# A five-layer graph network on one core: six turned blocks of the adjacency matrix are turned again on VectorE instead of being stored

## The chip, the core and the metric

The kernel runs on one core of one Trainium2 chip. The metric is the device time of one execution in microseconds (us). "PE" is TensorE, "DVE" VectorE, "ACT" ScalarE, "POOL" GpSimd and "SP" SyncE; SP does nothing here but issue transfers and wait for the semaphores before them.

## What is computed

A chain of four layers on x (5120 nodes by 64 features) with a dense 5120 by 5120 matrix adj, all in float32:

```
h = relu(layernorm(x));  x = x + L0(h): e = (weights and diagonal applied to h) + h
                                        layernorm(adj @ (adj.T @ e)) * gamma + beta + h
h = relu(layernorm(x));  x = x + adj @ h                                   # L1
h = relu(layernorm(x));  T1 = adj @ h; T2 = 2 adj @ T1 - h; T3 = 2 adj @ T2 - T1
                         x = x + h W0 + T1 W1 + T2 W2 + T3 W3 + b          # L2
h = relu(layernorm(x));  x = x + relu(d (adj + I) d (h W + b)), d = degree ** -0.5   # L3
```

adj is 105 MB and doesn't fit on the chip. A product adj @ v contracts over the columns of adj, so TensorE needs it turned (columns on the partitions).

## The kernel before

**First stage.** adj is read once, in seven groups of columns (six of 768, one of 512), ten blocks of 512 rows each, into `raw`. TensorE uses each block for adj.T @ e (`products_for_t`, L651) and turns it 128 by 128 with an identity (`turn_banks`, L673); ScalarE copies the turned banks into `staged` (`copy_banks`, L879). Of the six 128-wide chunks of a pair of blocks VectorE turns the last (`turn_chunk`, L1129), with instructions of 32 by 256 that each turn 32 by 32 squares. The turned pair (3 MB: three tiles of 1 MB) serves for the second product of L0 (`product_for_h`) and is stored to `adj_t` in DRAM (`store`, L570). The last group stays on the chip as far as it fits.

**Five passes.** The rest is five products with adj: one for L1, three for L2, one for L3. A tile (m, k) is 256 columns k by 1024 rows m, turned: 1 MB, in one of the slots of `whole`. A pass has 5 rows m of 20 tiles. A tile costs TensorE 8 matmul instructions (`multiply`, L640), and one that is loaded is used for the next pass too, as a "dual", where the features of that pass are ready in time. `Plan` writes this out by hand as 334 steps: in each the own tile, the small matmuls that belong to the ends of rows, then the duals of the step. All engines run through the same steps, each in its own order, and meet only at semaphores. 305 tiles are used and 295 of these loaded, in plan order, by SP (`load_turned`, L588); a load waits until the tile that was in its slot has been multiplied. `Plan` gives a tile the slot that comes free first. Fifteen slots rotate, some of them available only later: `over_wide` (slot 0), ten of `over_last` and four in `staged`; three more serve once. Eight tiles (`AT_START`) are loaded before the passes begin, the first of them into slot 0.

**Ends of rows.** A row that ends with its own tile at step e is finished by VectorE: at step e+1 it copies the sum out of the bank (L1243 with a part, L1245 without) and turns it with 16 small transposes (L1169), except in the fourth pass and in the last row of all, where TensorE does that (L799) and waits for the copy. At e+2 the result goes into x or into the features of the next pass (L1215, L1221, L1226, L1229 to L1234). After the passes of L1 and L2's last product a normalisation follows: at e+3 and e+4 on VectorE, ScalarE and POOL (the last instruction of it is L1203 in the first pass), then for the first pass L809 on TensorE at e+7 and a copy on ScalarE (L995) in the same step, and two batches of weights on TensorE (L825) at e+8 and e+9, which VectorE reads (L1184, L1188) and ScalarE too (L1005). TensorE doesn't begin the second batch before the first has been read. For the fourth pass these come at e+5 and e+6 (L809, L831, L1194, L1197).

How soon features are used is fixed by `READY = [11, 4, 4, 8, None]`: a row of pass p that ended at step e has its features ready for pass p+1 at step e + READY[p], and TensorE waits for `rows_ready` there.

Of the kernel before, what the change touches and what calls it, by code (L numbers as in the profile page):

```python
# [10 lines left out]
P = 128  # L11
# [28 lines left out]
SLOTS = EARLY_SLOTS + NB + LATE_SLOTS  # L40
KEPT = CHUNKS_LAST // 2
ONCE = SLOTS + KEPT
AT_START = [0] + list(range(EARLY_SLOTS + NB, SLOTS)) + [ONCE] + list(range(EARLY_SLOTS + NB - KEPT, EARLY_SLOTS + NB))
OPEN_BANKS = 5
EPS = 1e-5
SQ = 32
# [20 lines left out]
WEIGHED = (0, 3)  # L67
KEPT_FROM = 12
EARLY_FROM, EARLY_EVERY, EARLY_ROWS = 2, 2, 2


def kept_slot(m, j):
# [4 lines left out]
class Plan:  # L77


    def __init__(self):  # L80
# [114 lines left out]
        for n, (p, m, k, _) in enumerate(self.tiles):  # L195
            if p == 0 and k >= COLS - KEPT:
                self.slot[n] = kept_slot(m, k - (COLS - KEPT))
                if m >= 1:
                    empty.append((self.used_no(n), self.slot[n], n))
        loads_of = {}  # L200
        for n in range(len(self.tiles)):
            if n not in self.slot:
                place = min(empty, key=lambda x: x[0])
                empty.remove(place)
                _, j, self.slot_before[n] = place
                loads_of[j] = loads_of.get(j, 0) + 1
                self.slot[n], self.load_no[n] = j, loads_of[j]
                self.loads.append(n)
                if j != ONCE:
                    empty.append((self.used_no(n), j, n))  # L210

    def early_in_row(self, order, m, left, step, ready, covered):

# [23 lines left out]
def gnn_stack(nc, x_d, adj_d, wu_d, du_d, pu_d, wi_d, di_d, pi_d, gam_d, bet_d, w2_d, b2_d, w3_d, b3_d, out_d):  # L237
    plan = Plan()
    ctx = ExitStack()
    with ctx:  # L240
# [3 lines left out]
        def sem(name):  # L244
            return ctx.enter_context(nc.semaphore(name))
# [50 lines left out]
        over_c12 = [c12_flat[:, j * TILE_WORDS:(j + 1) * TILE_WORDS] for j in range(KEPT)]  # L296
        over_y = staged[:, LATE_SLOTS * TILE_WORDS:(LATE_SLOTS + 1) * TILE_WORDS]
        whole = [w[:, :] for w in over_wide + over_last] + over_staged + over_c12 + [over_y]
        out_rows = sq
        C1, C2 = C12[:, 0], C12[:, 1]  # L300

# [19 lines left out]
        early_in = sem("early_in")  # L321
        late_in = sem("late_in")
        weights_ready = sem("weights_ready")
        x_in = [sem(f"x_in{i}") for i in range(len(X_PARTS))]
        diag_in = sem("diag_in")
        diag_turned = sem("diag_turned")
# [44 lines left out]
        pool_step = sem("pool_step")  # L371

        adj_v = adj_d.rearrange("(m a p) k -> p m a k", a=SUB, p=P)
        x_v = x_d.rearrange("(t p) d -> p t d", p=P)
        out_v = out_d.rearrange("(m a p) d -> p m a d", a=CH, p=P)
        FEATURES = [R, E, C2, C1, R]
# [36 lines left out]

        def wait_loaded(eng, n):

            if n in plan.load_no:
                eng.wait_ge(whole_in[plan.slot[n]], 16 * plan.load_no[n])

        def chunks(g):
# [129 lines left out]
        @block.sync  # L549
        def _(sp):  # L550
            def load_x(i):
                t = slice(X_PARTS[i][0] * SUB, X_PARTS[i][1] * SUB)
                sp.dma_start(X[:, t, :], x_v[:, t, :]).then_inc(x_in[i], 16)

            def load_first(m):
                sp.dma_start(raw[:, m], adj_v[:, m, :, 0:GW]).then_inc(raw_in[m], 16)

            load_x(0)
            sp.dma_start(diag_rows[0:U // P, :], du_d.rearrange("(t p) -> t p", p=P)).then_inc(diag_in, 16)
            sp.dma_start(diag_rows[U // P:NT, :], di_d.rearrange("(t p) -> t p", p=P)).then_inc(diag_in, 16)  # L560
            load_x(1)
            load_first(0)
            load_x(2)
            for m in range(1, NB):
                load_first(m)

            def store(g, m):
                wait_copied(sp, g, m)
                at = g * CHUNKS * PAIR
                sp.dma_start(adj_t[m, :, at:at + STAGE_WORDS], staged_pair(g, m)).then_inc(stored_by(g, 2 * m)[0], 16)  # L570

            def store_kept(u):
                wait_copied(sp, NG - 1, u // 2, u % 2)
                at = (NG - 1) * CHUNKS * PAIR + u % 2 * TILE_WORDS
                sp.dma_start(adj_t[u // 2, :, at:at + TILE_WORDS], turned_into(NG - 1, u)).then_inc(stored_by(NG - 1, u)[0], 16)

            def load_next(g, m):

                wait_turned(sp, g, m // 2)
                wait_summed(sp, g, m)  # L580
                src = adj_v[:, m, :, (g + 1) * GW:(g + 1) * GW + chunks(g + 1) * P]
                sp.dma_start(raw_of(g + 1, m), src).then_inc(raw_in[m], 16)

            def load_turned(n):

                p, m, k, dual = plan.tiles[n]
                j = plan.slot[n]
                sp.dma_start(whole[j], adj_t[m, :, k * TILE_WORDS:(k + 1) * TILE_WORDS]).then_inc(whole_in[j], 16)  # L588

            def first_load(n):  # L590
                p, m, k, dual = plan.tiles[n]
                g = (2 * k + 1) // CHUNKS
                for u in (2 * m, 2 * m + 1):
                    sp.wait_ge(*stored_by(g, u))
# [12 lines left out]
            first = iter(plan.loads[:len(AT_START)])  # L607
            first_load(next(first))
            sp.wait_ge(*stored_by(NG - 2, UNITS - 3))
            sp.wait_ge(used, unit_no(NG - 2, UNITS - 2))  # L610
            for _ in range(STAGE_WORDS // TILE_WORDS):
                first_load(next(first))
            store_kept(0)
            store_kept(1)
            sp.wait_ge(*stored_by(NG - 2, UNITS - 1))
            sp.wait_ge(used, unit_no(NG - 1, 0))
            for _ in range(LATE_SLOTS + 1 - STAGE_WORDS // TILE_WORDS):
                first_load(next(first))
            for u in range(2, UNITS):
                if u == UNITS - 1:  # L620
                    wait_turned(sp, NG - 1, u // 2)
                    wait_summed(sp, NG - 1, u)
                    for n in first:
                        first_load(n)
                store_kept(u)
            for u in range(UNITS - 2, UNITS):
                sp.wait_ge(*stored_by(NG - 1, u))
            sp.wait_ge(used, TOTAL_UNITS)
            for n in plan.loads[len(AT_START):]:
                sp.wait_ge(multiplied, plan.used_no(plan.slot_before[n]))  # L630
                load_turned(n)
# [216 lines left out]
        def _(act):  # L848
# [129 lines left out]
                group(g)  # L978
            last_group()

            for s in range(N_STEPS):
                if UNITS + s <= END_V:
                    end_of_layer(UNITS + s)
# [24 lines left out]
                for r in plan.row_at(s, 4, 4):  # L1008
                    p, m = plan.rows[r]
                    act.wait_ge(out_ready, m + 1)  # L1010
                    act.dma_start(out_v[:, m], out_rows[m % 2][:, :, :]).then_inc(out_stored[m % 2], 16)
            for i in range(2):
                act.wait_ge(out_stored[i], 16 * len(range(i, ROWS, 2)))

# [2 lines left out]
        def _(dve):  # L1017
# [143 lines left out]
            def turn_squares(r):  # L1161
# [8 lines left out]
                                                       src[q * SQ:(q + 1) * SQ, :, b, :])  # L1170
                last.then_inc(y_squares, 1)

            for s in range(N_STEPS):
                if UNITS + s <= END_V:
                    end_of_layer(UNITS + s)
# [59 lines left out]
                for r in plan.row_at(s, 1, *range(PASSES)):  # L1235
                    p, m = plan.rows[r]
                    dve.wait_ge(multiplied, plan.own_no[plan.last_own[p, m]])
                    if r - 2 in BY_TENSOR:
                        dve.wait_ge(y_rows, BY_TENSOR.index(r - 2) + 1)
                    bank = open_bank[plan.bank["own", p, m]]  # L1240
                    if (p, m) in plan.part_no:
                        dve.wait_ge(part_saved, plan.part_no[p, m] + 1)
                        ins = nc.vector.tensor_tensor(y_sb[r % 2], bank, part[:, m, :], ALU.add)  # L1243
                    else:
                        ins = nc.vector.tensor_copy(y_sb[r % 2], bank)  # L1245
                    ins.then_inc(y_saved, 1)
                    if r in BY_VECTOR:
                        dve.wait_ge(y_saved, r + 1)
                        turn_squares(r)


        @block.gpsimd
# [70 lines left out]
```

## Time and profile before

| | |
|---|---|
| median of 3 runs | 1450.26 us (1450.21 to 1451.71) |
| the profiled execution: its time, and the span in its trace | 1449.24 us, 1447.0 us |
| busy: PE, DVE, ACT, POOL | 1419.3 us (98%), 491.5 us (34%), 399.7 us (28%), 84.2 us (6%) |
| mean granted clock of TensorE | 0.999 of full speed |
| moved by DMA | 523.26 MB, mean 362 GB/s |
| first stage, five passes | 0 to about 549 us, 549 to 1447 us |

The span goes from the first to the last instruction; the time has some 2 us more around it. Busy shares are means over two stages that differ. Matmuls are pipelined and their ends modelled, so a busy PE isn't proof of a PE at its peak: the waits and the chain of work that ended last say who held whom.

### The profile page before, as it was taken

What the parts mean: (1) busy time and instruction counts of PE and PEld (TensorE: products, weight loads), DVE (VectorE), ACT (ScalarE), POOL (GpSimd) and SP (SyncE); (2) the same over time, 40 slices, a digit from 0 to 9 for tenths busy, and PEclk for the clock granted to TensorE, in tenths of its full rate; (3) what the DMA queues carried; (4) which work ended last, traced back from release to release, by engine and by line L of the source; (5) the groups of instructions that cost most, each with busy time, mean ns of one, the idle gap of its engine ahead of it and who ended that gap; (6) DMA issues with size and microseconds to landing.
All of it is one profiled execution on the core that took longest, in us unless ns stands there. A gap on an engine that the chain in (4) does not pass through costs nothing.

```text
span 1447.0 us, 18473 instructions
## 1 busy us (share of the span) xinstructions
PE 1419.3 (98%) x7601; PEld 600.1 (41%) x7601; DVE 491.5 (34%) x1082; ACT 399.7 (28%) x885; POOL 84.2 (6%) x67
## 2 busy tenths in 40 slices
PE   6999999999999999999999999999999999999998
PEld 3555555555555563333333333333333333333332
DVE  6684544545546533331132211011311121101044
ACT  2378777777776551000000000000000000000000
POOL 2210000000000037000000000000000000000000
PEclk9999999999999999999999999999999999999999
DMA  9999999999999998999996797899797848996998
GB/s 322 392 417 411 420 412 414 419 408 415 401 406 372 388 403 348 419 421 420 420 413 217 315 361 291 327 350 319 302 340 263 311 180 354 393 382 224 357 420 315
DMA packets 97607, 523.26 MB, mean 362 GB/s; under 512 B 18764, under 2 KB 18804, under 8 KB 54644
## 3 DMA queue, kind: packets, MB, share of 16 engines
q1 hardware_dynamic: 90436, 520.40, 91.3%
q10 hardware_dynamic: 7088, 1.67, 0.5%
q8 instruction: 61, 1.00, 0.3%
q14 instruction: 22, 0.18, 0.0%
HBM read 415.88 MB, written 106.17 MB: 361 GB/s over the span
## 4 chain that ended last, share of the span: by engine, by line
PE 61%; DMA 2%; DVE 1%; POOL 0%; issue 0%; ACT 0%; DVEq 0%
PE turned L640 33%; PE acc L640 25%; DMA over_wide<-adj_t 2%; PE turned L673 1%; PE turned L825 1%; PE t_rows L809 0%; PE turned L831 0%; DVE staged L1169 0%; PE t_acc L799 0%; PE t_acc L725 0%; PE t_rows L725 0%; POOL rstd L1272 0%; DVE staged L1035 0%; DVE staged L1025 0%; DVE staged L1231 0%
## 5 line engine op out<-in xcount | busy, mean ns | idle before, releaser
L1129 DVE STREAM_TRANSPOSE staged<-raw 32x256 f32<-32x256 f32 x448 | 194.9, 435 | 5.8
L651 PE MATMUL t_acc<-raw,E 128*64 128x384 f32 (+1 forms) x1120 | 184.4, 476 | 5.7 <-DMA raw<-in_adj_dram 5.7
L879 ACT ACTIVATE staged<-turned 128x512 f32<-128x512 f32 x303 | 152.7, 640 | 105.7 <-PE turned L673 105.2
L923 ACT ACTIVATE t_t<-raw 128x768 uint8<-128x768 f32 (+1 forms) x216 | 177.2, 902 | 0.0
L640 PE MATMUL acc<-staged,t_cur 128*64 128x512 f32 x720 | 161.1, 596 | 0.0
L673 PE MATMUL turned<-ident,raw 128*128 128x128 f32 x1376 | 160.2, 274 | 0.0
L673 PEld LDWEIGHTS turned<-ident,raw 128*128 128x128 f32 x1376 | 149.7, 140 | 24.9 <-issue 24.9
L640 PE MATMUL turned<-over_last,C 128*64 128x512 f32 x672 | 152.1, 592 | 0.0
L651 PEld LDWEIGHTS t_acc<-raw,E 128*64 128x64 f32 x1120 | 78.3, 138 | 109.4 <-issue 86.0
L1272 POOL TENSOR_TENSOR rstd<-rstd,minus_half 128x8 f32<-128x8 f32 (+1 forms) x30 | 44.2, 1473 | 1267.1 <-DVE rstd L1031 1267.1
L640 PE MATMUL turned<-over_last,R 128*64 128x512 f32 x512 | 116.5, 593 | 0.0
L640 PE MATMUL acc<-over_last,R 128*64 128x512 f32 x440 | 99.9, 593 | 0.0
L987 ACT ACTIVATE part<-turned 128x512 f32<-128x512 f32 x12 | 7.2, 597 | 313.1 <-PE turned L640 287.3
L1169 DVE STREAM_TRANSPOSE staged<-staged 32x128 f32<-32x128 f32 x304 | 91.9, 302 | 4.5
L640 PEld LDWEIGHTS turned<-over_last,C 128*64 128x64 f32 x672 | 48.2, 137 | 95.5 <-issue 95.5
L1083 DVE TENSOR_TENSOR h_acc<-acc,h_acc 128x512 f32<-128x512 f32 x30 | 20.8, 692 | 197.2 <-PE acc L640 197.2
L640 PEld LDWEIGHTS acc<-staged,t_cur 128*64 128x64 f32 x720 | 49.0, 137 | 90.8 <-issue 90.8
L640 PE MATMUL acc<-over_last,C 128*64 128x512 f32 x384 | 86.6, 592 | 0.0
L1243 DVE TENSOR_TENSOR staged<-turned,part 128x512 f32<-128x512 f32 x11 | 7.6, 692 | 225.8 <-PE turned L640 191.7
L640 PE MATMUL turned<-over_last,E 128*64 128x512 f32 x320 | 74.1, 593 | 0.0
L640 PEld LDWEIGHTS turned<-over_last,R 128*64 128x64 f32 x512 | 36.2, 137 | 71.2 <-issue 69.4
L855 ACT ACTIVATE staged<-staged 128x512 f32<-128x512 f32 x10 | 6.3, 630 | 206.0 <-DVE staged L1025 206.0
(139 smaller groups left out, 1062.9 us busy)
## 6 DMA issues: line engine op xcount, KB each, us to landing
over_last<-adj_t SPq DMA_DIRECT2D x181, 1024.0 KB, 8.9
staged<-adj_t SPq DMA_DIRECT2D x91, 1024.0 KB, 9.5
raw<-in_adj_dram SPq DMA_DIRECT2D x60, 1536.0 KB, 19.7
adj_t<-staged SPq DMA_DIRECT2D x30, 3072.0 KB, 18.1
over_wide<-adj_t SPq DMA_DIRECT2D x23, 1024.0 KB, 7.6
raw<-in_adj_dram SPq DMA_DIRECT2D x10, 1024.0 KB, 14.8
adj_t<-over_last SPq DMA_DIRECT2D x8, 1024.0 KB, 12.1
adj_t<-C SPq DMA_DIRECT2D x2, 1024.0 KB, 21.7
```

The costliest lines, as they stand in the source:

```text
L640: last = nc.tensor.matmul(bank[h * D:(h + 1) * D, :], v[:, t + c, :], tile[:, (2 * c + h) * B:(2 * c + h + 1) * B], start=start and c == 0 ...
L651: last = nc.tensor.matmul(t_acc[h * D:(h + 1) * D, 0:columns], E[:, m * SUB + a, :], raw_of(g, m)[:, a, h * columns:(h + 1) * columns], st ...
L673: last = nc.tensor.transpose(turned[n % TURN_BANKS][:, a * P:(a + 1) * P], raw_of(g, 2 * m + b)[:, sub, c * P:(c + 1) * P], ident[:, :])
L825: last = nc.tensor.matmul(weigh_bank[odd][:, i * 4 * D:(i + 1) * 4 * D], feat_t[rows, nodes], w0123[rows, :, :].rearrange("p w d -> p (w d ...
L879: nc.scalar.activation(turned_into(g, u)[:, i * B:(i + 1) * B], turned[n % TURN_BANKS][:, :], ACT.Copy) \
L923: nc.scalar.activation(passed[n % 2][:, 0:chunks(g) * P], raw_of(g, m)[:, a, :], ACT.Copy, accum_out=deg_part[:, m * SUB + a, g:g + 1]).th ...
L987: nc.scalar.activation(part[:, m, :], open_bank[plan.bank["dual", p, m]], ACT.Copy).then_inc(part_saved, 1)
L1083: ins = nc.vector.tensor_tensor(h_acc[:, m, :], acc[pair % 2][:, :], h_acc[:, m, :], ALU.add)
L1129: last = nc.vector.transpose(dst[b * SQ:(b + 1) * SQ, :, :, q * SQ:(q + 1) * SQ], src[q * SQ:(q + 1) * SQ, :, :, c * P + b * SQ:c * P + (b ...
L1169: last = nc.vector.transpose(dst[b * SQ:(b + 1) * SQ, :, h, e, :], src[q * SQ:(q + 1) * SQ, :, b, :])
L1243: ins = nc.vector.tensor_tensor(y_sb[r % 2], bank, part[:, m, :], ALU.add)
L1272: op.tensor_tensor(v, v, minus_half[:, t(0)], ALU.pow).then_inc(pow_ready, 1)
```

## The change

Six tiles, (m, k) = (2, 2), (4, 5), (3, 8), (4, 11), (3, 14) and (4, 17), each the last third of a stored pair, are left out of the store. TensorE, ScalarE and VectorE still turn them in the first stage, for the second product of L0. Where a pass has such a tile to load, ScalarE's queue loads two raw blocks of adj (1024 rows by 128 columns, 512 KB each, in rows of 512 bytes) into two rooms, and VectorE turns them into the tile's slot: 16 transposes a block, in four "quarters" of four, which `place_turning` assigns to steps, two quarters a step at most and none in the three steps after the end of a row. The rooms lie in `over_wide`, so slot 0 is gone for tiles, fourteen slots rotate and seven tiles are loaded ahead.

```diff
-AT_START = [0] + list(range(EARLY_SLOTS + NB, SLOTS)) + [ONCE] + ...
+AT_START = list(range(EARLY_SLOTS + NB, SLOTS)) + [ONCE] + ...
+UNSTORED = [(2, 2), (4, 5), (3, 8), (4, 11), (3, 14), (4, 17)]
+QUARTERS = 4
+QUARTERS_A_STEP = 2
+ROOM_LANDS, ROOM_AHEAD = 3, 6
...
-                loads_of[j] = loads_of.get(j, 0) + 1
-                self.slot[n], self.load_no[n] = j, loads_of[j]
-                self.loads.append(n)
+                self.slot[n] = j
+                if self.tiles[n][1:3] in UNSTORED:
+                    raws.append(n)
+                    self.turned_no[n] = 2 * len(raws)
+                else:
+                    loads_of[j] = loads_of.get(j, 0) + 1
+                    self.load_no[n] = loads_of[j]
+                    self.loads.append(n)
...
+    def place_turning(self, raws):
...
+        row_ends = {s + i for s in self.ended for i in (1, 2, 3)}
+        self.rooms_in, self.quarters_in, ends = {}, {}, []
+        for n in raws:
+            free = step_of[self.slot_before[n]][-1]
+            for c in range(2):
+                asked = max([free - ROOM_AHEAD] + [x + 1 for x in ends[-2:-1]])
+                self.rooms_in.setdefault(asked, []).append((n, c))
+                s = max([asked + ROOM_LANDS, free + 1] + ends[-1:])
+                q = 0
+                while q < QUARTERS:
+                    if s not in row_ends and len(self.quarters_in.get(s, [])) < QUARTERS_A_STEP:
+                        self.quarters_in.setdefault(s, []).append((n, c, q))
+                        q += 1
+                    else:
+                        s += 1
+                ends.append(s)
...
+        rooms = [over_wide[0][:, c * ROOM_WORDS:(c + 1) * ROOM_WORDS] for c in range(2)]
...
             def wait_loaded(eng, n):
-            if n in plan.load_no:
+            if n in plan.turned_no:
+                eng.wait_ge(room_turned, plan.turned_no[n])
+            elif n in plan.load_no:
...
             def store(g, m):
-                wait_copied(sp, g, m)
-                at = g * CHUNKS * PAIR
-                sp.dma_start(adj_t[m, :, at:at + STAGE_WORDS], staged_pair(g, m))...
+                at, words = g * CHUNKS * PAIR, STAGE_WORDS
+                if (m, (g + 1) * CHUNKS // 2 - 1) in UNSTORED:
+                    words = STAGE_WORDS - TILE_WORDS
+                    ... (waits for the banks of these words alone)
+                sp.dma_start(adj_t[m, :, at:at + words], staged_pair(g, m)[:, 0:words])...
...
             first = iter(plan.loads[:len(AT_START)])
-            first_load(next(first))
...
+            def load_room(n, c):                                  # on ScalarE, last in its step
+                p, m, k, dual = plan.tiles[n]
+                job = plan.turned_no[n] - 2 + c
+                if job >= 2:
+                    act.wait_ge(room_turned, job - 1)
+                at = k * 2 * P + c * P
+                act.dma_start(rooms[c].rearrange("p (r k) -> p r k", k=P),
+                              pair_v[:, m, :, at:at + P]).then_inc(room_in[c], 16)
...
+            def turn_room(n, c, q):                               # on VectorE, last in its step
+                if q == 0:
+                    dve.wait_ge(room_in[c], 8 * plan.turned_no[n])
+                    if c == 0:
+                        dve.wait_ge(multiplied, plan.used_no(plan.slot_before[n]))
+                src = rooms[c].rearrange("p (a h k) -> p h a k", h=2, k=P)
+                dst = whole[plan.slot[n]][:, c * PAIR:(c + 1) * PAIR].rearrange("p (h a n) -> p h a n", h=2, a=SUB)
+                for b in range(4):
+                    last = nc.vector.transpose(dst[b * SQ:(b + 1) * SQ, :, :, q * SQ:(q + 1) * SQ],
+                                               src[q * SQ:(q + 1) * SQ, :, :, b * SQ:(b + 1) * SQ])
+                if q == QUARTERS - 1:
+                    last.then_inc(room_turned, 1)
```

## Rows read from the trace of the kernel before

**Rows 1.** Windows: us, busy PE, PEld, DVE, ACT, POOL, granted clock, DMA share, GB/s.

```profile
216.00:252.00 36.00, 36.00 (x226) 18.66 (x224) 16.62 (x38) 29.11 (x68) 0.00 (x0) 1.00 1.02 411
612.00:648.00 36.00, 35.85 (x172) 12.02 (x168) 10.64 (x28) 2.59 (x5) 1.64 (x1) 1.00 1.01 420
```

**Rows 2.** Waits of PE over the span: total us, times, longest.

```profile
PE t_acc L651 <- DMA raw<-in_adj_dram: 5.7, 16, 1.0
...
PE acc L640 <- DMA over_wide<-adj_t: 0.2, 1, 0.2
```

**Rows 3.** Chain of work that ended last, first pass: start us, us, what.

```profile
581.75 14.55 DMA over_wide<-adj_t
...
648.45 0.41 PE turned L825
...
699.68 0.41 PE turned L825
...
700.75 39.63 PE acc L640 x184
...
757.78 0.41 PE turned L825
...
798.62 0.66 PE t_rows L809 x4
...
801.14 0.41 PE turned L825
```

**Rows 4.** Timeline of SP's queue where the passes begin.

```profile
555.15 0.32 SPq L588 DMA_DIRECT2D over_wide<-adj_t  x1
```

**Rows 5.** DMA of the last 67 us (1380 to 1447), ScalarE's queue.

```profile
q10 hardware_dynamic: 5200, 1.31, 8.6%
```

**Rows 6.** Costliest groups: count, busy us, mean ns of one, idle before.

```profile
L1129 DVE STREAM_TRANSPOSE staged<-raw 32x256 f32<-32x256 f32 x448 | 194.9, 435 | 5.8
```

**Rows 7.** Timeline of DVE, ends of four rows of the first pass.

```profile
642.66 0.68 DVE L1203 TENSOR_TENSOR X<-X,b 128x512 f32<-128x512 f32 x1
...
692.57 0.68 DVE L1203 TENSOR_TENSOR X<-X,b 128x512 f32<-128x512 f32 x1
...
750.67 0.68 DVE L1203 TENSOR_TENSOR X<-X,b 128x512 f32<-128x512 f32 x1
...
798.48 0.68 DVE L1203 TENSOR_TENSOR X<-X,b 128x512 f32<-128x512 f32 x1
```

**Rows 8.** Timeline of DVE, passes two to four.

```profile
1007.52 0.68 DVE L1222 SCALAR_TENSOR_TENSOR X<-staged,X 128x512 f32<-128x512 f32 x1
1014.89 0.69 DVE L1243 TENSOR_TENSOR staged<-turned,part 128x512 f32<-128x512 f32 x1 [6.68 <-PE turned L640]
...
1157.98 0.69 DVE L1226 SCALAR_TENSOR_TENSOR C<-staged,C 128x512 f32<-128x512 f32 x1
...
1245.15 0.69 DVE L1243 TENSOR_TENSOR staged<-turned,part 128x512 f32<-128x512 f32 x1 [27.93 <-PE turned L640]
```

**Rows 9.** Chain of work that ended last, fourth pass.

```profile
1167.58 0.59 PE t_acc L799 x4
...
1246.82 0.59 PE t_acc L799 x4
```

**Rows 10.** Timeline of DVE, last pass.

```profile
1382.61 0.69 DVE L1197 TENSOR_TENSOR R<-R,dis 128x512 f32<-128x512 f32 x1
...
1393.07 5.04 DVE L1169 STREAM_TRANSPOSE staged<-staged 32x128 f32<-32x128 f32 x16
...
1440.41 0.69 DVE L1243 TENSOR_TENSOR staged<-acc,part 128x512 f32<-128x512 f32 x1 [1.55 <-PE acc L640]
```

**Rows 11.** Windows, last 3 us, columns as in rows 1.

```profile
1444.00:1447.00 3.00, 0.00 (x0) 0.00 (x0) 0.00 (x0) 0.00 (x0) 0.00 (x0) 0.50 0.38 87
```

**Rows 12.** Timeline of PE at the start of the kernel.

```profile
17.48 4.22 PE L651 MATMUL t_acc<-raw,E 128*64 128x384 f32 x16
...
22.44 2.80 PE L651 MATMUL t_acc<-raw,E 128*64 128x384 f32 x16
```

More of the change, by code:

```diff
@@ L42 @@
 ONCE = SLOTS + KEPT
-AT_START = [0] + list(range(EARLY_SLOTS + NB, SLOTS)) + [ONCE] + list(range(EARLY_SLOTS + NB - KEPT, EARLY_SLOTS + NB))
+AT_START = list(range(EARLY_SLOTS + NB, SLOTS)) + [ONCE] + list(range(EARLY_SLOTS + NB - KEPT, EARLY_SLOTS + NB))
 OPEN_BANKS = 5
@@ L69 @@
 EARLY_FROM, EARLY_EVERY, EARLY_ROWS = 2, 2, 2
+UNSTORED = [(2, 2), (4, 5), (3, 8), (4, 11), (3, 14), (4, 17)]
+ROOM_WORDS = CH * P
+QUARTERS = 4
+QUARTERS_A_STEP = 2
+ROOM_LANDS, ROOM_AHEAD = 3, 6
 def kept_slot(m, j):
@@ L200, in __init__ @@
         loads_of = {}
+        self.turned_no, raws = {}, []
         for n in range(len(self.tiles)):
@@ L205, in __init__ @@
                 _, j, self.slot_before[n] = place
-                loads_of[j] = loads_of.get(j, 0) + 1
-                self.slot[n], self.load_no[n] = j, loads_of[j]
-                self.loads.append(n)
+                self.slot[n] = j
[6 more added lines that the diff above has]
+                    self.loads.append(n)
                 if j != ONCE:
                     empty.append((self.used_no(n), j, n))
+        self.place_turning(raws)
+    def place_turning(self, raws):
+        step_of = {}
+        for s, n in enumerate(self.step_tile):
+            for x in [n] * (n is not None) + self.duals_in.get(s, []):
+                step_of.setdefault(x, []).append(s)
+        row_ends = {s + i for s in self.ended for i in (1, 2, 3)}
[14 more added lines that the diff above has]
+                ends.append(s)
+            assert ends[-1] + 2 <= step_of[n][0], (self.tiles[n], ends[-1], step_of[n])
     def early_in_row(self, order, m, left, step, ready, covered):
@@ L323, in gnn_stack @@
         weights_ready = sem("weights_ready")
+        room_in = [sem(f"room_in{c}") for c in range(2)]
+        room_turned = sem("room_turned")
         x_in = [sem(f"x_in{i}") for i in range(len(X_PARTS))]
@@ L373, in gnn_stack @@
         adj_v = adj_d.rearrange("(m a p) k -> p m a k", a=SUB, p=P)
+        pair_v = adj_d.rearrange("(m r p) k -> p m r k", r=CH, p=P)
         x_v = x_d.rearrange("(t p) d -> p t d", p=P)
@@ L567, in store @@
             def store(g, m):
-                wait_copied(sp, g, m)
-                at = g * CHUNKS * PAIR
-                sp.dma_start(adj_t[m, :, at:at + STAGE_WORDS], staged_pair(g, m)).then_inc(stored_by(g, 2 * m)[0], 16)
+                at, words = g * CHUNKS * PAIR, STAGE_WORDS
+                if (m, (g + 1) * CHUNKS // 2 - 1) in UNSTORED:
+                    words = STAGE_WORDS - TILE_WORDS
+                    sp.wait_ge(chunk_copied, COPIED_NO[g, m, words // B - 1])
+                    if (g, m, MOVED_BANK) in MOVED_NO:
+                        sp.wait_ge(bank_moved, MOVED_NO[g, m, MOVED_BANK])
+                else:
+                    wait_copied(sp, g, m)
+                sp.dma_start(adj_t[m, :, at:at + words], staged_pair(g, m)[:, 0:words]).then_inc(stored_by(g, 2 * m)[0], 16)
             def store_kept(u):
@@ L979, in _ @@
             last_group()
+            def load_room(n, c):
[4 more added lines that the diff above has]
+                at = k * 2 * P + c * P
+                act.dma_start(rooms[c].rearrange("p (r k) -> p r k", k=P), pair_v[:, m, :, at:at + P]).then_inc(room_in[c], 16)
             for s in range(N_STEPS):
@@ L1011, in _ @@
                     act.dma_start(out_v[:, m], out_rows[m % 2][:, :, :]).then_inc(out_stored[m % 2], 16)
+                for n, c in plan.rooms_in.get(s, []):
+                    load_room(n, c)
             for i in range(2):
@@ L1249, in _ @@
                         turn_squares(r)
+                for n, c, q in plan.quarters_in.get(s, []):
+                    turn_room(n, c, q)
         @block.gpsimd
```

## Prediction

> **What bounds the kernel now.** The windows come first [rows 1]. In the first stage (216 to 252 us) the DMA engines are full, 411 GB/s at a share of 1.02, and TensorE is busy for all 36 us; early in the passes (612 to 648) the DMA is as full (420 GB/s) and TensorE busy 35.85 of 36. Two resources are at their limit at once, so busy shares don't say who holds whom. The waits do [rows 2]: TensorE stood for raw blocks 5.7 us in the whole run, in 16 pieces, for a turned tile 0.2 us in the row shown. TensorE is the bound, and the DMA is only just quick enough. How just, the chain shows [rows 3]: it runs through TensorE's matmuls, but at 581.75 it leaves them for a transfer of 14.55 us, whose landing lets TensorE go on. There a tile lands as it is needed; slack grows later. The same chain gives the unit: 184 matmuls in 39.63 us are 23 tiles, 1.72 us a tile. VectorE looks free (10.64 of 36 us in the second row of [rows 1]), but its work comes in clumps at the ends of rows, and there TensorE needs it: at 798.62 the chain [rows 3] steps from VectorE's last work to TensorE's L809 without a gap.
>
> **First stage.** Six of 30 stores lose 1 MB of 3. No instruction of TensorE goes, since all six tiles are still turned there. The DMA is relieved of 6 x 1.049 MB / 411 GB/s = 15.3 us [rows 1], but TensorE can get back only what it stood for: 5.7 us [rows 2]. I take -5.0, bounds 0 and -5.7.
>
> **Loads in the passes.** The planner's rules, followed in the code, replace 18 of 295 loads by 36 raw blocks. Two things press on the stretch without slack. First, slot 0 is gone: one tile fewer is loaded ahead, and since the stream of the passes starts at 555.15 as before [rows 4] (SP stands there for its last stores), 1 MB more must pass before each tile: 1.049 / 420 GB/s = 2.5 us. Second, the raw blocks of the first turning, (2, 2), are asked at step 38, which ScalarE reaches after its work of step 28, some 10 steps ahead of its slot; their MB passes before tiles that have no slack. Their price isn't in the trace: by bytes 2.5 us; by the 256-byte rows of the output, 8.6% of 16 x 67 us / 5200 = 17.7 ns a packet [rows 5], two such for each 512 bytes, 2048 x 35 / 16 ns = 4.5 us. A line through 17.7 ns and the 312 ns of an 8 KB packet at 420 GB/s gives 27 ns, 3.5 us, which I take since it leans on the nearer row. Together +6.0, bounds 2.5 (raw blocks absorbed) and 9. The Trainium skill (DMA: Bandwidth & Descriptors, Specifications) puts the least transfer at line rate at 512 bytes; by that the blocks would cost 2.5 us and the sum 1 us less. No run here shows it yet.
>
> **VectorE's price.** The new transposes have the shape of L1129, 32 by 256, 435 ns each [rows 6]: 16 a block, 6.96 us; 32 a tile, 13.92 us; 18 tiles 250 us, on an engine that is two thirds idle. But two quarters a step are 3.48 us, against 1.72 us for a step of one tile, and VectorE works in order: the end of a row waits behind every quarter of an earlier step. The planner spares only steps e+1 to e+3. Where steps hold an own tile and a dual (3.44 us) nothing happens. The other places, in order, with the times of before:
>
> - **Steps 48 and 68.** Four quarters stand between the end of normalisation (L1203) and VectorE's reading of the first batch, which TensorE needs for its second. L1203 ends at 643.34 and 693.25 [rows 7]; plus 6.96 and 0.95 for the reading: 651.25 and 701.2, where TensorE wants to go on at 648.45 and 699.68 [rows 3]. +2.8 and +1.5.
> - **Step 88.** Here eight quarters, those of tile (4, 11), lie in steps 83 to 86, between the same two. The quarters of steps 76 to 79 delay VectorE by 1.8 us, which the slack of the row nearly hides (0.2). L1203's end at 751.35 [rows 7] + 13.92 + 1.0 = 766.3, against 757.78 [rows 3]: 8.5, and with the 1.8 delay less the stall 0.2 already counted, +10.0 in all.
> - **Steps 106, 107.** Quarters in steps 98 and 99 need 6.96 us; the row's last tile is done 3 tiles (5.15 us) after they can start: 1.8 late, and L809 at 798.62 has no slack. Then the four of steps 103 and 104 follow L1203 (799.16 [rows 7] + 1.8) and end at 807.9. ScalarE, in step 105, waits for that very turning before it asks the next raw block, and the copy that L825 needs is behind it: 807.9 + 0.7 = 808.6 against 801.14 [rows 3] + 1.8. +1.8 and +5.6.
> - **Step 117.** With quarters in 107 to 110 the end of the next row starts 2.2 us late; its 0.3 of slack leaves +2.0.
> - **Step 180.** Eight quarters in steps 173 to 176, one tile each. VectorE is free for them at 1008.2 and would end at 1022.1; the row's copy stood at 1014.89 [rows 8]. 7.2 late, and the four tiles (6.9 us) that cover its 6.5 us of turning are the whole slack. +7.2.
> - **Step 224.** The same in steps 220 to 223: from 1158.67 [rows 8] to 1172.6, then a copy of 0.7: 1173.3. TensorE itself waits for it at L799, at 1167.58 [rows 9]. +5.8.
> - **Step 247.** Steps 241 to 244, started 6 tiles before the row's copy at 1245.15 [rows 8], at 1234.8: 1248.7 + 0.7 against 1246.82 [rows 9]. +2.6.
> - **The end.** From 1383.3 [rows 10] VectorE has three tiles to turn (41.8 us), four rows to finish at 0.7 + 5.04 + 3 x 0.7 = 7.9 us (31.6) and the last row's 6.6 us (1440.41 to 1447.0): 1463.3, where all of it lay beside TensorE before. TensorE meanwhile waits some 10 us for its last tile, inside this. +16.3.
>
> VectorE's sum: 2.8 + 1.5 + 10.0 + 7.4 + 2.0 + 7.2 + 5.8 + 2.6 + 16.3 = 55.6 us.
>
> **TensorE's clock.** It fell to 0.50, 1.2 GHz, in the last 3 us, when TensorE had nothing left [rows 11], so four stalls of over 5 us (88, 107, 180, 224) should bring it down. Coming back costs, by the first 16 matmuls of L651 after a thin stretch, 4.22 - 2.80 = 1.4 us [rows 12]: +5.6; bounds 0 and twice that, if those 16 were slow throughout.
>
> **Hidden.** ScalarE's 36 issues cost nothing where it waits anyway; without that cover 36 x 0.32 (SP's issue [rows 4]) = 11.5 us. SP has 18 issues fewer; its in-order waits gain nothing, since slots come free at TensorE's pace.
>
> Sum: -5.0 + 6.0 + 55.6 + 5.6 = 62.2. The profiled execution took 1449.24, so 1511.4; the median is 1.0 above it: 1512.
>
> **Rivals.** (1) *Not slower: VectorE's turning fits.* It decides at the price of a quarter: at 0.86 us, two in a step of one tile, VectorE keeps pace, the stalls at 88, 180 and 224 vanish and the end is covered. Then -5.0 + 6.0 is left, 1451, and with the bounds 5.7 and 2.5 taken, 1447. For it speaks that VectorE idles two thirds of the run; against it, 448 instructions of the same shape at 435 ns, twice that price [rows 6]. The Trainium skill (VectorE: DVE Perf Modes, The three transpose paths) gives 311 ns for 128 by 128 in bf16, an estimated 5.0 us for a tile's 16 such squares, and by that this rival would hold; the trace, in float32, says 13.92. (2) *Part of the lateness is absorbed:* stalls move TensorE behind, so that later clumps find VectorE ahead, or duals fill the gaps. With steps 88, the end and half of the others: 10.0 + 16.3 + 14.6 + 1 = 42, 1492; with no clock loss and the end halved, 1484. For it: one wait can hide another, as at step 224; against: the places lie 40 us and more apart, each with its own clump. (3) *The raw blocks land late.* VectorE then stands in order before a quarter. They are asked at least 3 steps (5.2 us) ahead; a full DMA took 14.55 us [rows 3]. If half of the 18 came 4 us late on the path, +36: 1548. Against it: nearly all are asked while VectorE is still busy with the block before, 7 us.
>
> **Chances.** Forecast 0.75; (1) 0.05; (2) 0.12; (3) 0.08. The likeliest gives 1512. Its own bounds: 1450.3 + 55.6 - 2.8 (step 48 absorbed) - 5.7 + 2.5 = 1500, and 1450.3 + 55.6 + 9 + 11.2 = 1526. With parts of (2) and (3): 1488 to 1535, which leaves out (1), the lower half of (2) and most of (3). A measurement tells 0.2% (3 us) from no change. Slower takes all of the forecast, (2) and (3), 0.95; (1) is split, 0.03 same and 0.02 faster.
>
> **What would show it.** Some 576 transposes of 32 by 256 at 435 ns, VectorE busy near 740 us; waits of L651 for raw blocks under 1 us; waits of TensorE for VectorE's new transposes, near 10 us at the last tile, and for the readings before L825 (10 us), for ScalarE's copy (5 to 6), at L799 (6) and for C at the duals of step 180 (7); the last 60 us full on VectorE. A wait for a raw block behind VectorE would be rival (3). The prediction is wrong if quarters are cheaper than 435 ns allow, or if the planner's order of VectorE isn't what I read.

## The result, and the profile after

The change makes the kernel slower: 1552.86 us against 1450.24 on the same chip (medians of four runs each), a ratio of 1.0705 with a 95% interval of 1.0692 to 1.0717. The forecast was 1512, its range 1488 to 1535; 62.2 us more were forecast and 102.6 came.

The profiled execution of the changed kernel took 1555.73 us, 106.5 more than that of before; its span is 1553.9 us and the mean granted clock 0.968 (before: 1447.0 and 0.999). The page comes first: busy time of the engines, two groups of instructions (operation, count, busy us, mean ns, idle time before them), and two kinds of transfer (count, size, median us to landing). Line numbers have moved: L640 is now L689, L651 L700, L799 L848, L809 L858, L825 L874, L1005 L1063, L1243 L1317; L1242 is the new turning, L1037 the new load.

```profile
PE 1443.3 (93%) x7601; PEld 606.0 (39%) x7601; DVE 743.0 (48%) x1658; ACT 400.0 (26%) x885; POOL 84.3 (5%) x67
...
L1242 DVE STREAM_TRANSPOSE over_last<-over_wide 32x256 f32<-32x256 f32 x416 | 181.3, 436 | 92.8 <-PE turned L689 67.0
...
L1242 DVE STREAM_TRANSPOSE staged<-over_wide 32x256 f32<-32x256 f32 x160 | 69.8, 436 | 46.9 <-DMA over_wide<-in_adj_dram 44.7
...
over_wide<-in_adj_dram ACTq DMA_DIRECT2D x36, 512.0 KB, 7.9
adj_t<-staged SPq DMA_DIRECT2D x6, 2048.0 KB, 15.5
```

The 576 transposes take 436 ns each, and VectorE is busy 743.0 us, both as forecast. TensorE issues the same 7601 matmuls, but is busy 24.0 us longer, and its idle time in the span (span less busy) went from 27.7 to 110.6 us: 82.9 + 24.0 = 106.9, the whole growth of the span. So there are two things to explain, waits and slower matmuls. First the waits. These are the waits of PE in the changed kernel (total us, times, longest), to be held against [rows 2]:

```profile
PE turned L689 <- DVE staged L1242: 14.7, 1, 14.7
PE t_acc L848 <- DVE staged L1317: 14.6, 3, 6.2
PE turned L874 <- ACT C L1063: 13.0, 3, 10.7
PE acc L689 <- DVE staged L1242: 11.2, 1, 11.2
PE acc L689 <- DVE over_last L1242: 9.4, 1, 9.4
PE acc L689 <- DVE C L1300: 7.6, 1, 7.6
PE t_rows L858 <- DVE staged L1095: 7.4, 3, 4.4
...
PE turned L874 <- ACT feat_t L1053: 5.1, 1, 5.1
PE t_acc L700 <- DMA raw<-in_adj_dram: 1.9, 2, 1.0
```

Most are the waits that were forecast. Two are not: the 11.2 us for a turned tile in the first pass (with 4.4 us behind it, at L858), and 14.7 beside the 9.4 near the end, where one wait of some 10 was expected. What VectorE did before those two, its timeline shows (start, us, instructions, in brackets the idle time before and what ended it):

```profile
674.22 7.18 DVE L1242 STREAM_TRANSPOSE staged<-over_wide 32x256 f32<-32x256 f32 x16 [16.86 <-DMA over_wide<-in_adj_dram]
694.02 7.18 DVE L1242 STREAM_TRANSPOSE staged<-over_wide 32x256 f32<-32x256 f32 x16 [12.62 <-DMA over_wide<-in_adj_dram]
...
1489.58 7.18 DVE L1242 STREAM_TRANSPOSE staged<-over_wide 32x256 f32<-32x256 f32 x16 [2.49 <-DMA over_wide<-in_adj_dram]
1509.45 7.18 DVE L1242 STREAM_TRANSPOSE staged<-over_wide 32x256 f32<-32x256 f32 x16 [12.69 <-DMA over_wide<-in_adj_dram]
```

VectorE stands for raw blocks four times, 44.7 us in all, and the turnings of the blocks that came late end where TensorE begins again. ScalarE's queue shows when these two blocks of the first pass were asked (the second line joins two issues, the first of which waits for nothing):

```profile
648.76 0.38 ACTq L1037 DMA_DIRECT2D over_wide<-in_adj_dram  x1
...
657.39 24.42 ACTq L1037 DMA_DIRECT2D over_wide<-in_adj_dram  x2
```

The block asked at 648.76 could be turned at 674.22, that of 657.39 at 694.02: 25 and 37 us, where the median block took 7.9 from issue to landing. The DMA queues from 657 to 695 us say why (packets, MB, share of 16 engines; q1 carries SP's loads of tiles, q10 the raw blocks of ScalarE's queue):

```profile
q1 hardware_dynamic: 1989, 14.48, 93.0%
q10 hardware_dynamic: 1988, 1.00, 9.2%
```

The two queues get the same number of packets, not of bytes: 1988 small ones and 1989 large ones. A small packet costs 9.2% x 16 x 38 us / 1988 = 28 ns, a large one 93.0% x 16 x 38 / 1989 = 284 ns. A raw block is 1024 rows of 512 bytes, 64 packets on each of 16 engines; if each waits for one large packet, a block takes an estimated 64 x (28 + 284) ns = 20 us. The two blocks came 19.8 us apart (674.22 and 694.02). The Trainium skill (DMA: Bandwidth & Descriptors, Queues, rings and completion order) says that an engine goes round its queues packet by packet; these rows agree.

TensorE's clock explains the rest. Windows around the wait before step 88's second batch, columns as in [rows 1]:

```profile
786.00:791.00 5.00, 0.00 (x0) 0.00 (x0) 4.83 (x12) 0.00 (x0) 0.00 (x0) 0.50 0.00 0
791.00:794.00 3.00, 2.02 (x10) 1.28 (x10) 0.80 (x4) 0.38 (x1) 0.00 (x0) 0.50 0.02 5
794.00:797.00 3.00, 3.00 (x10) 0.99 (x10) 0.89 (x4) 0.77 (x2) 0.00 (x0) 0.50 0.30 85
797.00:800.00 3.00, 3.00 (x14) 0.94 (x12) 0.00 (x0) 0.00 (x0) 0.00 (x0) 0.84 0.97 264
```

TensorE begins again at 791.98 and has 0.50, 1.2 GHz, until about 798; then 2.4 GHz come back. Matched one by one with those of the kernel before, the matmuls behind this wait are 3.0 us longer in sum. Behind each of ten waits of 2.2 to 14.7 us they are 1.3 to 3.2 us longer, 24.1 us together; behind the last wait of the run, which only four matmuls follow, 0.5; the rest of the run is 0.6 shorter. That is the 24.0.

### The profile page after: what moved, and what is told of

It is laid out like the page before. It is cut to its first block, busy times and chain, and to the rows that moved or that the text cites. A ratio compares the mean times of both kernels' runs of the same rounds, so it can differ in the third digit from the quotient of the medians.

```text
span 1553.9 us, 19071 instructions
## 1 busy us (share of the span) xinstructions
PE 1443.3 (93%) x7601; PEld 606.0 (39%) x7601; DVE 743.0 (48%) x1658; ACT 400.0 (26%) x885; POOL 84.3 (5%) x67
## 4 chain that ended last, share of the span: by engine, by line
PE 43%; DVE 15%; DMA 8%; issue 1%; POOL 0%; ACT 0%; ACTq 0%; DVEq 0%
PE turned L689 22%; PE acc L689 19%; DVE over_last L1242 7%; DMA over_wide<-in_adj_dram 5%; DVE staged L1242 3%; DMA staged<-adj_t 3%; DVE staged L1229 3%; PE turned L722 1%; PE turned L874 1%; POOL rstd L1348 0%; PE turned L880 0%; DVE staged L1317 0%; PE t_acc L848 0%; PE t_rows L858 0%; DVE staged L1319 0%
## 5 line engine op out<-in xcount | busy, mean ns | idle before, releaser
L1242 DVE STREAM_TRANSPOSE over_last<-over_wide 32x256 f32<-32x256 f32 x416 | 181.3, 436 | 92.8 <-PE turned L689 67.0
L700 PE MATMUL t_acc<-raw,E 128*64 128x384 f32 (+1 forms) x1120 | 182.4, 477 | 1.9 <-DMA raw<-in_adj_dram 1.9
L689 PE MATMUL acc<-staged,t_cur 128*64 128x512 f32 x720 | 161.1, 596 | 0.0
L689 PE MATMUL turned<-over_last,C 128*64 128x512 f32 x632 | 142.8, 592 | 0.0
L689 PE MATMUL turned<-over_last,R 128*64 128x512 f32 x560 | 131.3, 604 | 1.5 <-DMA over_last<-adj_t 1.5
L689 PE MATMUL acc<-over_last,R 128*64 128x512 f32 x472 | 112.7, 612 | 10.2 <-DVE over_last L1242 9.4
L700 PEld LDWEIGHTS t_acc<-raw,E 128*64 128x64 f32 x1120 | 79.7, 138 | 101.9 <-issue 90.9
L689 PE MATMUL acc<-over_last,C 128*64 128x512 f32 x480 | 111.2, 604 | 1.2 <-DVE C L1295 1.2
L1242 DVE STREAM_TRANSPOSE staged<-over_wide 32x256 f32<-32x256 f32 x160 | 69.8, 436 | 46.9 <-DMA over_wide<-in_adj_dram 44.7
L689 PE MATMUL acc<-staged,R 128*64 128x512 f32 x312 | 73.8, 610 | 12.4 <-DVE staged L1242 11.2
L689 PE MATMUL turned<-over_last,E 128*64 128x512 f32 x352 | 84.7, 612 | 0.0
L689 PEld LDWEIGHTS acc<-staged,t_cur 128*64 128x64 f32 x720 | 48.9, 137 | 90.8 <-issue 90.8
L689 PE MATMUL turned<-staged,C 128*64 128x512 f32 x360 | 83.1, 593 | 0.0
## 6 DMA issues: line engine op xcount, KB each, us to landing
adj_t<-staged SPq DMA_DIRECT2D x6, 2048.0 KB, 15.5
```

The source lines that it names most:

```text
L689: last = nc.tensor.matmul(bank[h * D:(h + 1) * D, :], v[:, t + c, :], tile[:, (2 * c + h) * B:(2 * c + h + 1) * B], start=start and c == 0 ...
L700: last = nc.tensor.matmul(t_acc[h * D:(h + 1) * D, 0:columns], E[:, m * SUB + a, :], raw_of(g, m)[:, a, h * columns:(h + 1) * columns], st ...
L1242: last = nc.vector.transpose(dst[b * SQ:(b + 1) * SQ, :, :, q * SQ:(q + 1) * SQ], src[q * SQ:(q + 1) * SQ, :, :, b * SQ:(b + 1) * SQ])
```

## Experiments

The edits of E1 and E2 are to the kernel before, those of E3 to E9 to the changed kernel; E8 tries for a version that gains. In the text, "against before" is the ratio to the kernel before on the same chip, with its 95% interval. The chips differ a little: the kernel before took 1450.24 us on the chip of the result, 1450.66 on that of E1 to E4, 1452.07 on that of E5 to E7 and 1450.58 on that of E8 and E9.

**E1 and E2: what the first stage gives, what the slot costs.** E1 keeps the short stores alone; the passes load tiles with slot 0 as before, and for an unstored tile its stored neighbour. E2 has fourteen slots and seven tiles ahead, with full stores and no turning.

```diff
# E1, to the kernel before
+UNSTORED = [(2, 2), (4, 5), (3, 8), (4, 11), (3, 14), (4, 17)]
...                                   (store as in the change)
+                k -= (m, k) in UNSTORED
                 sp.dma_start(whole[j], adj_t[m, :, k * TILE_WORDS:(k + 1) * TILE_WORDS])...
# E2, to the kernel before
-AT_START = [0] + list(range(EARLY_SLOTS + NB, SLOTS)) + [ONCE] + ...
+AT_START = list(range(EARLY_SLOTS + NB, SLOTS)) + [ONCE] + ...
...
-            first_load(next(first))
```

> The kernel before with the six short stores alone; slot 0, the eight loads ahead and SP's loads stay, and where a pass needs one of the six tiles SP loads its stored neighbour, so that part of the products is taken from other columns. If TensorE is the bound of the first stage, only its waits for raw blocks (5.7 us) can come back: 1445 to 1447, the waits of L651 under 2.5 us, the first tile of the passes 3 to 5 us earlier. Rival, the first stage is bound by the DMA: 15 us less, 1435.

> The kernel before with fourteen slots in place of fifteen and seven tiles loaded ahead, nothing else. By the forecast's term 2.5 us more (1452.7), as waits of TensorE for turned tiles in the first 80 us of the passes. Rival, the slot was spare: no change, 1450.3.

E1 took 1440.93 us, 0.9936 (0.9923 to 0.9949) against before: 9.7 us less, more than the 5.7 that was set as the bound. E2 took 1454.37, 1.0024 (1.0015 to 1.0034): 3.7 more, but not where it was expected. At the tile that the kernel before begins at 641.09 us TensorE is 0.7 us late in E2's trace; 3.1 more are lost in the last 17 us, where it waits for the last tiles to land (timeline of PE):

```profile
1436.42 1.94 PE L639 MATMUL acc<-over_last,R 128*64 128x512 f32 x8 [0.45 <-DMA over_last<-adj_t]
1439.76 1.94 PE L639 MATMUL acc<-staged,R 128*64 128x512 f32 x8 [1.41 <-DMA staged<-adj_t]
1442.34 1.94 PE L639 MATMUL acc<-over_last,R 128*64 128x512 f32 x8 [0.64 <-DMA over_last<-adj_t]
```

The DMA share from 1430 to 1440 us is 1.03 there and was 0.77 before.

The bound of E1 had been read from the waits of the matmuls. The waits of the weight loads of the same line tell more; first the kernel before, then E1 (there the line is L659):

```profile
PEld t_acc L651 <- DMA raw<-in_adj_dram: 17.8, 21, 1.5
```

```profile
PEld t_acc L659 <- DMA raw<-in_adj_dram: 6.5, 10, 1.5
```

These fell by 11.3 us, those of the matmuls from 5.7 to 2.6, and PE's busy time by 2.4: part of the waiting had stood in the profile as long matmuls. The profiled execution of E1 was 1444.19, 5.1 under that of before and the longest of E1's five. The first stage's gain varies: at the first matmul of the passes TensorE is 3.9 us ahead of before in the trace of E1, and from 3.7 (E7) to 8.4 (E4) in those of the other kernels with six short stores. What E1's other runs gained no trace shows.

**E4 and E3: the landing of the raw blocks.** E4 asks the two rooms once; every later turning reads these first blocks, so that VectorE's work is the same and its order too, but nothing lands late. With it go 34 transfers of 512 KB, which pass before tiles in the changed kernel, and ScalarE's waits before them. E3 keeps all loads with their bytes and steps, but takes them from the stored neighbour, in rows of 4 KB instead of 512 bytes.

```diff
# E4
                 if job >= 2:
-                    act.wait_ge(room_turned, job - 1)
+                    return
...
-                    dve.wait_ge(room_in[c], 8 * plan.turned_no[n])
+                    dve.wait_ge(room_in[c], 16)
# E3
-                at = k * 2 * P + c * P
-                act.dma_start(rooms[c].rearrange("p (r k) -> p r k", k=P), pair_v[:, m, :, at:at + P])...
+                at = (k - 1) * TILE_WORDS + c * PAIR
+                act.dma_start(rooms[c], adj_t[m, :, at:at + PAIR])...
...                                   (ScalarE waits once for the last stores)
```

> The changed kernel, but the two rooms are loaded once, before the first turning; the later turnings use what lies there, so the turned tiles hold other columns. If late landings of raw blocks made what the forecast lacks, the waits at step 64 (11.2 and 4.4 us), half of the last 33 us and the clock lost there go: 1553 falls to about 1515, and TensorE's waits for VectorE in the order of steps stay as they were (10.7 at step 88, 7.6 at step 180, 6.2 at step 224). Rival, VectorE alone is late: 1550.

> The changed kernel with the same 36 loads of 512 KB on the same queue at the same steps, but from stored tiles, whose rows are 4 KB instead of 512 bytes, so the turned tiles hold other columns. If the two queues take turns packet by packet (1989 and 1988 packets from 657 to 695 us), a block passes with 1 MB of the other queue beside it instead of 8 MB, lands within 8 us where it took 25 to 45, and the time is near that with one load, 1515 to 1522. Rival, ScalarE's queue is served late whatever it carries, or the rooms are asked too late: 1545 to 1553.

E4 took 1514.58, 1.0444 (1.0428 to 1.0460): 38.3 us less than the changed kernel. VectorE waits for no raw block, and the waits that VectorE's order makes all stay (10.7 before step 88's second batch, 7.6 at the duals of step 180, 6.2 for the fourth pass's copies). Of its 42.2 us of span, 10.8 are PE's busy time. In its timeline of PE the end is near the forecast, 11.44 + 4.90 = 16.3 us of waiting, of which the kernel before had 0.8:

```profile
1496.86 3.68 PE L689 MATMUL acc<-over_last,R 128*64 128x512 f32 x8 [11.44 <-DVE over_last L1242]
1505.44 1.11 PE L848 MATMUL t_acc<-ident,staged 128*128 128x128 f32 x4 [4.90 <-DVE staged L1317]
```

E3 took 1525.29, 1.0517 (1.0496 to 1.0538): 27.6 less than the changed kernel, with the same bytes, though 3 us above what was expected. Its queues from 644 to 660 us:

```profile
q1 hardware_dynamic: 847, 6.15, 92.5%
q10 hardware_dynamic: 143, 0.52, 8.2%
```

One block (0.52 MB) is now in 143 packets beside 847, and landed in 9.1 us there; VectorE's waits for blocks fell from 44.7 to 3.7 us (waits of DVE; L1244 is the turning there):

```profile
DVE over_last L1244 <- DMA over_wide<-adj_t: 3.7, 2, 3.3
```

So it is the number of packets in a queue that has to take turns, not the bytes, that made the blocks late. Of the 10.7 us between E3 and E4 the traces show where: TensorE waits 2.8 us longer in E3 for its last turned tile (14.2 against 11.4; a block was there only 18.4 us after ScalarE came to ask for it), 4.7 us for the copy of step 107, where ScalarE waits for a room first (E4 waits 1.9 a batch later instead), and is busy 7.2 us longer. How much of it is late landing was not tested.

**E5, E6, E7: single places.** E5 moves the quarters of tile (4, 11) in the first pass from steps 83 to 86 to steps 89 to 92. E6 turns nothing in the last pass and loads the stored neighbours there. E7 fills three of the waits with matmuls on the identity that nothing reads, so that TensorE stays busy: 88 before the tile of step 64, 84 before the second batch of step 88, 58 before the duals of step 180.

```diff
# E5
+                s = max([asked + ROOM_LANDS, free + 1] + ends[-1:] + [89] * (self.tiles[n][:3] == (0, 4, 11)))
# E6
+                if self.tiles[n][1:3] in UNSTORED and self.tiles[n][0] < PASSES - 1:
...
+                k -= (m, k) in UNSTORED
# E7
+            FILL = {64: 88, 88: 84, 180: 58}
+            def fill(s, at):
+                for i in range(FILL[s] if s == at else 0):
+                    nc.tensor.transpose(t_acc[:, i % SUB * P:(i % SUB + 1) * P], ident[:, :], ident[:, :])
...                                   (called at the three places)
```

> The changed kernel with the eight quarters of tile (4, 11) in the first pass in steps 89 to 92 instead of 83 to 86; nothing else. If VectorE's order makes the wait at step 88, its 10.7 us go, and with them some 3 us in which TensorE ran at half clock behind it: 1539. If the clock costs only the 1.4 us of the forecast: 1541. Rival, the lateness is only moved to the next row: 1550 to 1553.

> The changed kernel without the three turnings of the last pass: there SP loads a stored neighbour of the tile, so part of the last product is taken from other columns. From L831 of step 294 to the end the changed kernel took 33 us more than the kernel before; if VectorE's work and the late blocks there are all of it, 1553 falls by 31 to 33, to 1521. Rival, the last pass is late because the passes before it leave VectorE behind: falls by less than 20.

> The changed kernel, with TensorE turning the identity into a free bank where it otherwise stands: 88 times before tile 64, 84 before the second batch of step 88, 58 before the duals of step 180, 0.107 us each, 1 to 2 us less than each wait. It adds work and takes none away. If a wait costs clock, the granted clock stays at 1.00 through the three places, the matmuls behind them take 1.72 us a tile at once, and the time falls by 2 to 3 us a place, 5 to 8 in all: 1545 to 1548, TensorE's other busy time 5 to 8 us lower. Rival, the 24 us that TensorE is busy longer come from slower operands (transfers and VectorE beside it): no change, 1553.

E5 took 1544.74, 8.1 less than the changed kernel; 12 to 14 were expected. The 10.7 us before step 88's second batch are gone, which shows their cause; but TensorE now waits 3.3 us for that tile itself, and 6.4 instead of 5.1 for the copy of step 107. E6 took 1524.74, 28.1 less (31 to 33 expected): the last pass holds over a quarter of the loss. (Measured from the kernel before on each chip, E5, E6 and E7 are 10.0, 30.0 and 6.1 us less than the changed kernel, 1.8 more than the times alone say.)

E7 took 1548.63, 4.2 less. Around step 88 its clock is 1.00 in all four windows where the changed kernel had 0.50 and 0.84:

```profile
786.00:791.00 5.00, 5.00 (x49) 5.00 (x47) 4.83 (x13) 0.00 (x0) 0.00 (x0) 1.00 0.00 0
791.00:794.00 3.00, 1.61 (x15) 1.20 (x13) 1.84 (x6) 0.38 (x1) 0.00 (x0) 1.00 0.00 0
794.00:797.00 3.00, 3.00 (x16) 1.06 (x16) 0.89 (x4) 0.77 (x2) 0.00 (x0) 1.00 0.27 75
797.00:800.00 3.00, 3.00 (x16) 1.01 (x14) 0.00 (x0) 0.00 (x0) 0.00 (x0) 1.00 1.00 275
```

The same eight matmuls after the wait take 1.94 us instead of 3.68; first the timeline of the changed kernel, then that of E7:

```profile
793.98 3.68 PE L689 MATMUL turned<-over_last,R 128*64 128x512 f32 x8
```

```profile
782.29 9.39 PE L832 MATMUL t_acc<-ident 128*128 128x128 f32 x84
793.06 0.45 PE L882 MATMUL turned<-w,feat_t 64*128 64x256 f32 x1 [1.39 <-ACT C L1072]
...
794.13 1.94 PE L689 MATMUL turned<-over_last,R 128*64 128x512 f32 x8
```

Without the fill (25.8 us, the sum of its three groups) PE is busy 1432.8 us, 10.5 less than in the changed kernel, 3.5 a place. But only 4 to 6 come back in time: TensorE waits longer elsewhere (6.3 instead of 4.4 us in step 66, 6.4 instead of 5.1 in step 107). So the slow clock is the cause of the longer matmuls at these three places, and about half of that was the run's time.

**E9: the price of a quarter.** E4 with half of the transposes of each quarter left out, so that a quarter takes 0.87 us, the point from which rival (1) was to hold.

```diff
-                for b in range(4):
+                for b in range(2):
```

> The kernel with the rooms loaded once, and with two of the four transposes of each quarter left out, so half of each turned tile keeps what lay there: a quarter costs 0.87 us, the point from which the forecast's first rival should hold. By it the waits at steps 88, 180 and 224 vanish, the end is covered, and the time is 1450.5 less 9.7 for the stores plus 3.7 for the slot: 1445 to 1450. Rival, the waits are of another kind than VectorE's time in order: 1480 or more, half of the way back from 1515.

E9 took 1450.95, 0.9999 (0.9988 to 1.0011): the time of before, and 63.6 us less than E4, from which it differs in the transposes alone. Of the waits on VectorE's clumps one of 1.9 us and some smaller than a microsecond are left:

```profile
PE t_acc L700 <- DMA raw<-in_adj_dram: 2.8, 3, 1.4
PE turned L874 <- ACT C L1063: 1.9, 1, 1.9
PE acc L689 <- DMA staged<-adj_t: 1.9, 4, 0.8
```

So the slowness is VectorE's time and the blocks' landing (E4 and E9 take away the blocks' transfers as well); what is left of the change costs what it gives.

**E8: a version that might gain.** Two tiles instead of six, their turnings written into gaps of VectorE by hand, blocks asked 14 steps ahead, and slot 0 used for tiles until step 46, so that eight tiles are loaded ahead again.

```diff
+UNSTORED = [(3, 11), (4, 11)]
+PLACES = {(0, 3, 11): [70, 70, 71, 71, 72, 72, 73, 73],
+          (0, 4, 11): [83, 83, 83, 89, 89, 90, 90, 91],
...
+SLOT_0_UNTIL = 40
+ROOM_AHEAD = 14
```

> Two tiles instead of six, (3, 11) and (4, 11), six turnings in place of 18, none in the last 60 us; the quarters are put by a list into the stretches in which VectorE has nothing due (three of a block between L1203 and the first batch's reading at step 83, the rest behind the batches), the raw blocks are asked 14 steps ahead, and slot 0 serves for tiles until step 46, so that eight tiles are again loaded ahead. If order on VectorE, late landing and the lost slot are all that the change costs, nothing of it is left, TensorE waits for no transpose, and a part of what the short stores give (9.7 us for six) stays: 1443 to 1448. Rival, some of the cost is of another kind (the transposes or the small rows slow TensorE's own work): 1452 or more.

E8 took 1452.01, 1.0008 (0.9999 to 1.0017): no difference, where 1443 to 1448 was expected. That is the rival's time, but not its cause: PE is busy only 1.0 us longer than before. TensorE waits for no turning and VectorE for no block, so the places were right; but two short stores gave little. The waits of the weight loads for raw blocks (here L704) fell only from 17.8 to 14.7 us, and the matmuls' waits for tiles rose from 0.7 to 3.4:

```profile
PEld t_acc L704 <- DMA raw<-in_adj_dram: 14.7, 16, 2.0
```

```profile
PE acc L693 <- DMA over_last<-adj_t: 1.9, 3, 0.6
PE acc L693 <- DMA staged<-adj_t: 1.1, 2, 0.6
```

Its trace shows two places. TensorE is 0.6 us ahead at the first matmul of the passes and 0.6 late at the tile of 641.09; and 2.7 us go in the last 17, around waits for the last tiles, as in E2, where slot 0 is missing too.

No version was faster than the kernel before, except E1, which turns nothing.

## Why the prediction was right in direction and 41 us short

**Right: VectorE's order.** The ten places before the end were forecast at 39.3 us together, and PE's idle pieces there add up to 39.3. One by one, measured against forecast: step 48 1.7 (2.8), 68 0.6 (1.5), 88 with its L858 11.5 (10.0), 106 and 107 7.3 (7.4), 117 1.2 (2.0), 180 7.6 (7.2), 224 6.2 (5.8), 247 3.3 (2.6). The mechanism is right; that the two sums are equal is luck, since single places are off by up to 1.5. E5 shows the cause at step 88; E9, held against E4, that all of them hang on the price of a quarter. That of step 107 hung on ScalarE's issue in step 105, as read: E4, which waits for no room there, has no such wait for the copy (its waits for ScalarE's C are 3.2 us longer).

**Failed: the landing of the raw blocks.** The step is the one that set rival (3) aside: "nearly all are asked while VectorE is still busy with the block before", with 14.55 us as the time of a full DMA. So the sum has nothing for the landing. The price of a packet was nearly right (27 ns forecast, 28 measured), but it was put only into the loads; that each packet of 28 ns waits for one of 284 was not in it. Late landing is worth 27.6 us by E3, and at most 38.3 by E4 (10.8 of them longer matmuls), which also takes the blocks' transfers away; the result lies 40.9 above the forecast. Four blocks came 2.5 to 16.9 us after VectorE was ready, not nine by 4; two of the four in the first pass, where the DMA is full anyway [rows 1], two in the last, where its share was 1.02 and more from 1470 to 1510 us. Rival (3) had the right mechanism, and 8 in 100 was too little for it. That its 1548 is near 1552.86 is partly luck: its 36 us were nine blocks late by 4.

**What that did.** In the first pass 11.2 and 4.4 us, steps 64 and 66, of which the forecast had nothing. At the end 33.3 us instead of 16.3: TensorE was 73.6 us behind the times of before at the products of the fourth pass's last row, and 106.9 at the end (first the chain of before, then that of the changed kernel):

```profile
1380.76 1.09 PE turned L831 x8
```

```profile
1454.40 1.10 PE turned L880 x8
```

E4, without late blocks, loses 17.9 there, 15.5 of it in new waits.

**Too small: the clock.** +5.6 stood for four stalls of 1.4; there were ten waits with 1.3 to 3.2 us of longer matmuls behind each, 24.0 in all, and 13.2 even in E4. The 1.4 came from one group of 16 matmuls, and a stall slows more than the next 16. E7 shows that this is not all time: 4 to 6 us of 10.5 for three places.

**The first stage and the slot.** -5.0 was forecast, and the first matmuls of the passes came 4.8 us earlier in the changed kernel:

```profile
552.37 29.36 PE acc L640 x136
```

```profile
547.53 17.34 PE acc L689 x80
```

But the bound of -5.7 was wrong: the stores alone give 9.7 (E1). The slot cost 3.7 (E2), not 2.5, and most of it at the end of the run. In the changed kernel the waits for loaded tiles between 577 and 643 us rose from 0.7 to 3.3, and the lead of 4.8 us fell to 1.2 at the tile of 641.09: 3.6 us, against +6.0 for both loads.

**A sum that came out by luck.** E4's 1514.58 is near the forecast of 1512, but not because every term was right: the first stage gave more, and the clock and the slot cost more. And one sum of the prediction leaves a term out: rival (2)'s 42 us have no clock in them; with the 5.6 its 1492 would be 1498.

E9 has both the short stores and the lost slot, and E1's 9.7 less and E2's 3.7 more don't show in it as 6 us less. Its trace says where they went: TensorE is 4.7 us ahead at the first matmul of the passes and 0.5 late at the tile of 641.09, after 4.3 us of waits for tiles in a stretch where the DMA is full; by the end it is 3.4 late.

Open are the exact share of the clock in the run's time, how much of the 10.7 us between E3 and E4 is late landing, and E1's gain beyond its trace.

## What to carry to other kernels

A small transfer that must be in time beside a stream of large ones is priced by its packets and the packet of the other queue that each waits for, not by its bytes: long rows took 27.6 us off with the same bytes (E3), and in E8, which asked 14 steps ahead, VectorE waited for no block. Work for an idle engine is to be laid out step by step against its in-order queue; two thirds of idle time said nothing, since the new work fell into clumps at the ends of rows. Where a trace's matmul waits set a bound, the weight loads' waits are to be read beside them.

## What the runs showed of the hardware

- Two queues under load took turns packet by packet: 1988 packets of some 500 bytes beside 1989 of some 7.3 KB, 1.00 against 14.48 MB in 38 us. Two blocks of 512 KB could be turned 25 and 37 us after they were asked, the median of the run from issue to landing being 7.9.
- Packets of 512 bytes cost 28 ns each, which is 16 x 512 / 28 = some 290 GB/s, against 410 by the same sum for the large ones in the same stretch. The Trainium skill (DMA: Bandwidth & Descriptors, Specifications) puts the least transfer at line rate at 512 bytes; these rows don't agree.
- After waits the granted clock was 0.50 while TensorE was at work again: after 10.7 us at step 88 from 791.98 to about 798, after 7.6 us at the duals of step 180 from 1079 to 1085 (0.50 and 0.55, then 1.00), and after 2.2 us at step 106 (to 837.86) 0.50 from 839 to 842, then 0.95 to 845.
